# A transformer layer on one core: q loads, x's split, batch 1's reciprocals and step 30 put in another order

## The reference

```
h = layernorm(x)
q = h @ Wq (32 heads of 32);  k, v = h @ Wkv (one head of 32 each)
a = softmax(q k^T * scale + slopes * (pos_k - pos_q), causal) v
x = x + a @ Wo
w = (6-bit codes of qweight - zero_point) * scale
x = x + layernorm(x) @ w^T + bias
```

## Time and profile before

| | |
|---|---|
| median of 3 runs (range) | 864.13 us (860.87 to 867.29) |
| the profiled execution, its span | 865.46 us, 863.7 us |
| mean granted clock of TensorE | 0.979 of full |
| busy in the span: TensorE, VectorE, ScalarE, GpSimd | 824.9, 580.6, 379.6, 434.0 us |
| DMA | 126.35 MB, mean 146 GB/s |

### The profile page before, as it was taken

One profiled execution on the slowest core, in us unless ns is written; L12 is line 12 of the kernel. 1 busy time (PEld: TensorE's weight loads), 2 busy tenths in 40 slices (PEclk: granted clock), 3 DMA queues, 4 the chain that ended last, 5 costly groups with the idle time before them and its releaser, 6 DMA issues.

```text
span 863.7 us, 13629 instructions
## 1 busy us (share of the span) xinstructions
PE 824.9 (96%) x4616; PEld 591.6 (68%) x4616; DVE 580.6 (67%) x1582; ACT 379.6 (44%) x731; POOL 434.0 (50%) x320
## 2 busy tenths in 40 slices
PE   7999999989899999999999999995999999999988
PEld 4787878867655655565556555683887888888876
DVE  4866564656767878888888883215744878684876
ACT  3646436312466677667666664202411141041321
POOL 0000000000278888888888886425654378453555
PEclk9999999998999999999999999996999999999999
DMA  9767676594546545664566535234035532510112
GB/s 334 256 204 221 212 255 206 170 232 124 151 115 148 146 132 143 147 158 109 156 161 158 146 104 201 60 110 159 33 116 181 168 122 95 173 49 1 49 49 98
DMA packets 70860, 126.35 MB, mean 146 GB/s; under 512 B 7444, under 2 KB 16692, under 8 KB 70456
## 3 DMA queue, kind: packets, MB, share of 16 engines
q1 hardware_dynamic: 70640, 125.23, 49.1%
q10 hardware_dynamic: 152, 0.27, 0.1%
HBM read 86.13 MB, written 38.94 MB: 145 GB/s over the span
## 4 chain that ended last, share of the span: by engine, by line
PE 67%; DMA 11%; DVE 7%; POOL 5%; issue 4%; ACT 4%; SPq 1%; DVEq 0%; POOLq 0%; ACTq 0%
PE p_st L868 10%; PE p_s L839 9%; PE p_o L879 9%; PE p_o L892 4%; PE p_s L939 4%; PE p_s L940 4%; PE p_s L941 4%; DMA inv<-inv_d 3%; DMA inv_b<-inv_d 3%; PE p_st L963 2%; PE p_st L964 2%; PE p_o L785 2%; PE p_o L788 2%; PE p_o L786 2%; PE p_st L939 2%
## 5 line engine op out<-in xcount | busy, mean ns | idle before, releaser
L1377 DVE CUSTOM_DVE_ANT_0 spill<-p_s,mask 128x128 bf16<-128x128 f32 (+3 forms) x512 | 223.2, 482 | 56.9 <-PE p_s L839 54.9
L612 POOL TENSOR_SCALAR_AFFINE_SELECT pt<-pt 128x512 f32<-128x512 f32 x128 | 81.9, 652 | 276.0 <-ACT pt L1111 276.0
L1111 ACT ACTIVATE pt<-p_st 128x512 f32<-128x512 f32 (+1 forms) x352 | 178.3, 559 | 86.1 <-PE p_st L868 85.7
L839 PE MATMUL p_s<-kst,xt 98*128 98x128 f32 (+3 forms) x512 | 150.3, 332 | 7.1 <-DVE mx L1377 5.8
L868 PE MATMUL p_st<-xt,kst 100*128 100x512 f32 (+1 forms) x352 | 140.7, 405 | 3.3 <-ACT pt L1111 2.9
L839 PEld LDWEIGHTS p_s<-kst,xt 98*128 98x128 f32 x512 | 99.1, 195 | 21.3 <-DVE mx L1377 8.5
L619 POOL TENSOR_TENSOR pt<-pt 128x1536 f32<-128x1536 f32 x32 | 111.8, 3492 | 2.7
L868 PEld LDWEIGHTS p_st<-xt,kst 100*128 100x128 f32 x352 | 66.7, 190 | 39.2 <-DVE ml L1384 18.1
L879 PE MATMUL p_o<-pt,vst 128*32 128x512 f32 (+3 forms) x1024 | 89.9, 445 | 0.0
L625 POOL TENSOR_TENSOR pt<-pt 128x1024 f32<-128x1024 f32 x32 | 76.9, 2403 | 0.0
L785 PE MATMUL p_o<-xt,wqh 128*128 128x512 f32 x136 | 55.7, 410 | 1.7 <-DVE wql L1291 1.7
(11 more groups left out here) (202 smaller groups left out, 1657.8 us busy)
## 6 DMA issues: line engine op xcount, KB each, us to landing
xt<-qh_d SPq DMA_DIRECT2D x64, 256.0 KB
xs<-in_x_t_dram SPq DMA_DIRECT2D x32, 256.0 KB, 5.8
qh_d<-qh SPq DMA_DIRECT2D x32, 256.0 KB, 3.1
ql_d<-ql SPq DMA_DIRECT2D x32, 256.0 KB, 4.0
xt<-ql_d SPq DMA_DIRECT2D x32, 256.0 KB
o_d<-o_st SPq DMA_DIRECT2D x32, 256.0 KB, 2.3
ob<-o_d SPq DMA_DIRECT2D x32, 256.0 KB, 4.1
xin<-in_x_dram SPq DMA_DIRECT2D x14, 512.0 KB, 8.4
```

The costliest lines, as they stand in the source:

```text
L839: pe.matmul(scores_of(n), qst[s % 4][0:R_MAX, j, qb * P:(qb + 1) * P], kst[0:R_MAX, b * S:b * S + keys], start=True, stop=True).then_inc(s ...
L1111: act.activation(pt[s % 2][:, j:j + heads, PT_AT[kb]:PT_AT[kb] + KB_LEN[kb]], p_st[:, place(k) % 3, 0:heads * KB_LEN[kb]].rearrange("p (j ...
L1377: dve.tensor_tensor_reduce(spill[:, SPILL_AT[qb]:SPILL_AT[qb] + keys], scores_of(n), mask[:, S - keys:S], 1.0, LOWEST, ALU.add, ALU.max, m ...
```

## The change

- SP, last batch: one `load_q` ahead of the stores, the others ahead of those of m = 2, 4 and 6, and that of step 3 at m = 6 instead of in step 0.
- VectorE and ScalarE, m = 7 of the first three batches: parts 6 and 7 of x are centred and split ahead of the q tile.
- Last q tile: ScalarE takes step 0's first two exponentials before its cast; VectorE's subtraction moves behind four maxima.
- Step 30: products 5 and 6 to its start, the low parts and product 7 behind `max_low`; `o_high(7)` and `o_low(7)` to step 31.
- Batch 1's outputs: all eight products on VectorE, 8 to 13 in step 31, 14 and 15 behind three evictions; eight broadcasts, six into places of their own (`inv_1`, which lies elsewhere in memory), the first six issued in step 31. The product is written over the reciprocals, so that `ob` comes free sooner. GpSimd keeps `add_x2` alone.
- The load of `scal` ahead of the wait for the last reciprocals, which `deviation(0)` waits for instead of the cast of `share_r`.
- MEAN of batch 0 from behind o(1,0) to behind four parts of o(1,1); SQUARES of the last batch from behind f(3,1) to behind f(3,2).

```diff
...
         sb = tensors(ctx)
         x2 = [None, sb("x2_odd", [P, CK, S])]
-        dev = sb("dev", [P, S])
+        share_r = sb("share_r", [P, P], F32R)
         scal = sb("scal", [P, 3 * CK])
         zs = sb("zs", [P, CK])
-        share_r = sb("share_r", [P, P], F32R)
+        dev = sb("dev", [P, S])
         sb("unused", [P, 224])
         x2[0] = sb("x2_even", [P, CK, S])
+        with ExitStack() as early:
+            inv_1 = tensors(early)("inv_1", [P, CK, S])
         yh = sb("yh", [P, CK, S], F32R)
...
             o_b = tensors(early)("o_b", [P, CK, 2, S], F32R)
         wi = sb("wi", [P, CK, CK, P], F32R)
-        with ExitStack() as early:
-            inv_1 = tensors(early)("inv_1", [P, CK, S])
         yl = sb("yl", [P, CK, S], F32R)
         xc = sb("xc", [P, 3, S])
...
         o_in = [sem(f"o_in{i}") for i in range(4)]
         inv_in = [sem(f"inv_in{i}") for i in range(2)]
-        inv_1_in = [sem(f"inv_1_in{i}") for i in range(2)]
+        inv_1_in = [sem(f"inv_1_in{i}") for i in range(6)]
         o_norm, o_hi, o_lo = (sem(n) for n in ("o_norm", "o_hi", "o_lo"))
         tile_done, evicted = sem("tile_done"), sem("evicted")
...
             return x2[t % 2][:, m, :]
+        def own_place(k):
+            return {CK: 0, CK + 1: 1, CK + 2: 2, CK + 3: 3, CK + 6: 4, CK + 7: 5}.get(k)
         def inv_turn(k):
-            return k if k < CK + 2 else k - (CK - 2)
+            return k if k < CK else k - 4 if k < 2 * CK else k - 6
         def inv_at(k):
-            return inv_1[:, k - CK, :] if CK + 2 <= k < 2 * CK else inv_b[:, inv_turn(k) % 2, :]
+            return inv_b[:, inv_turn(k) % 2, :] if own_place(k) is None else inv_1[:, own_place(k), :]
         def inv_landed(k):
-            if CK + 2 <= k < 2 * CK:
-                return inv_1_in[(k - CK) // 4], 16
+            if own_place(k) is not None:
+                return inv_1_in[own_place(k)], 16
             return inv_in[inv_turn(k) % 2], 16 * (inv_turn(k) // 2) + 16
+        def o_normal_at(k):
+            return inv_at(k) if k // CK == 1 else ob[:, k % 4, :]
         def xc_at(t, m):
...
                     load_codes(2 * b)
                     sp.wait_ge(q_done, CK * LASTB)
-                    for s in range(3):
-                        load_q(s)
+                    load_q(0)
                 for m in range(CK):
                     if not more and m in (6, 7):
                         store_max(m - 6)
+                    if not more and m in (2, 4, 6):
+                        load_q(m // 2)
                     n = CK * b + m
                     rows, cols = slice(m * P, (m + 1) * P), slice(b * S, (b + 1) * S)
...
             def attend(s):
-                if s + 3 < STEPS:
+                if 0 < s and s + 3 < STEPS:
                     at_least(sp, st_done, NU * s)
                     load_q(s + 3)
...
                 for k in range(CK):
-                    if k < 7 and s == max(17 + 2 * k, 19):
+                    if k < 7 and s == (17 + k if k < 2 else 17 + 2 * k):
                         load_inv(k)
                     if s == (19 + 2 * k if k < 4 else 14 + 2 * k):
...
                 if s == STEPS - 1:
                     for k in range(CK, CK + 4):
+                        load_inv(k)
                         load_o(k)
-                    load_inv(CK)
-                    load_inv(CK + 1)
+                    load_inv(CK + 4)
+                    load_inv(CK + 5)
                 if s > 0:
                     store_o(s - 1)
...
                     sp.wait_ge(wo_lo, HALVES)
                 sp.wait_ge(o_out, 16 * k + 16)
-                at_least(sp, o_lo, k - 3)
+                if CK + 4 <= k < 2 * CK:
+                    sp.wait_ge(o_norm, k - 3)
+                elif 2 * CK <= k < 2 * CK + 4:
+                    sp.wait_ge(o_norm, 2 * CK)
+                else:
+                    at_least(sp, o_lo, k - 3)
                 sp.dma_start(ob[:, k % 4, :], o_d[P * g:P * g + P, b * S:(b + 1) * S]).then_inc(o_in[k % 4], 16)
...
                 sp.wait_ge(inv_out, 16 * (b + 1))
-                at_least(sp, o_norm, CK + 1 + k - 2 * CK if 2 * CK <= k < 2 * CK + 2 else k - 1)
+                if own_place(k) is not None:
+                    sp.wait_ge(st_done, NU * (STEPS - 1 if own_place(k) < 4 else STEPS))
+                elif 2 * CK <= k < 2 * CK + 2:
+                    sp.wait_ge(o_lo, k - 3)
+                else:
+                    at_least(sp, o_norm, k - 5 if CK <= k < 2 * CK else k - 1)
                 src = inv_d[b].rearrange("(j r) q -> j r q", j=4)[:, g:g + 1, :].to_broadcast([4, 32, S])
                 sp.dma_start(inv_at(k), src).then_inc(inv_landed(k)[0], 16)
-            def load_inv_1(half):
-                sp.wait_ge(pv_done, STEPS)
-                src = inv_d[1].rearrange("(j r) q -> j r q", j=4)[:, 4 * half:4 * half + 4, :].rearrange(
-                    "j (a g) q -> j a (g q)", a=1).to_broadcast([4, 32, 4 * S])
-                sp.dma_start(flat(inv_1[:, 4 * half:4 * half + 4, :]), src).then_inc(inv_1_in[half], 16)
             def load_wi(m):
...
             for s in range(STEPS):
                 attend(s)
+            load_o(CK + 4)
+            load_o(CK + 5)
+            load_inv(CK + 6)
+            load_inv(CK + 7)
+            load_o(CK + 6)
+            load_o(CK + 7)
             store_o(STEPS - 1)
-            load_inv_1(0)
-            load_inv_1(1)
-            for k in range(CK + 4, 2 * CK):
-                load_o(k)
             load_x2(1, 0)
             load_x2(1, 1)
+            sp.dma_start(scal[:, :], rows).then_inc(rows_in, 16)
             sp.wait_ge(inv_done, 16 * B)
             sp.dma_start(inv_d[B - 1, :, :], sums[:, :]).then_inc(inv_out, 16)
-            sp.wait_ge(inv_out, 16 * B)
-            sp.dma_start(scal[:, :], rows).then_inc(rows_in, 16)
             for k in range(2 * CK, 2 * CK + 4):
...
                 add(s, 1)
-            for k in range(CK, CK + 3):
-                o_normal(k)
-            add_x2(0, 1)
-            add_x2(0, 2)
-            for m in range(3, CK):
-                for k in (CK + 2 * m - 3, CK + 2 * m - 2):
-                    if k < 2 * CK:
-                        o_normal(k)
+            for m in range(1, CK):
                 add_x2(0, m)
             for t in (1, 2, 3):
...
             for t in (1, 2, 3):
                 for m in range(CK):
-                    out_tile(t, m)
-                    if (t, m) == (1, 0):
-                        over_features(0, MEAN)
+                    for c in range(CK):
+                        out_part(t, m, c)
+                        if (t, m, c) == (1, 1, 3):
+                            over_features(0, MEAN)
                     if m == 4:
                         over_features(t - 1, YSUM)
...
             for m in range(CK):
                 ffn_tile(LASTB, m)
-                if m == 1:
+                if m == 2:
                     over_features(LASTB, SQUARES)
...
                         act.activation(mv[:, 0, 3:4], eps[:, 0:1], ACT.Exp).then_inc(table_in, 1)
+                    if n == CK * B - 1:
+                        exponentials(0, 0)
+                        exponentials(0, 1)
+                    if more and m == CK - 1:
+                        for c in CENTRE[m]:
+                            x_high(b + 1, c)
                     act.wait_ge(q_freed, n + 1)
                     at_least(act, q_out[m % 2], 32 * (4 * b + m // 2))
...
                     if 0 < b < LASTB and m == TURN_M[b]:
                         take_stats(b + 1)
-                    if more:
+                    if more and m < CK - 1:
                         for c in CENTRE.get(m, ()):
                             x_high(b + 1, c)
...
                 if k == 0:
                     at_least(act, pv_done, s - 1)
+                    if s == 0:
+                        act.wait_ge(q_done, CK * B)
                 act.activation(pt[s % 2][:, j:j + heads, PT_AT[kb]:PT_AT[kb] + KB_LEN[kb]],
                                p_st[:, place(k) % 3, 0:heads * KB_LEN[kb]].rearrange("p (j q) -> p j q", j=heads),
...
                     if k == TURN_AT and 0 < s < STEPS - 1:
                         max_high(s + 1)
-                    exponentials(s, k)
+                    if (s, k) not in ((0, 0), (0, 1)):
+                        exponentials(s, k)
                     if k == 0 and s % GROUPS == 1 and s > GROUPS:
                         take_sums(s // GROUPS - 1)
...
                     if k == 3 and s in (21, 23, 25, 27, 29):
                         o_high((s - 21) // 2)
-                    if s == STEPS - 2 and k in (3, 6, 9):
+                    if s == STEPS - 2 and k in (3, 6):
                         o_high(k // 3 + 4)
+                    if s == STEPS - 1 and k == 3:
+                        o_high(7)
...
                 if k == 3 * CK:
                     act.wait_ge(tile_done, tile_at("o", 2, CK - 1) + 1)
```

(50 more changed lines are left out.)

## The result

The changed kernel took 832.32 us in the median of 4 runs (831.53 to 833.71), the kernel before 865.71 (860.87 to 868.90). The ratio is 0.9621, its 95% interval 0.957 to 0.9671. In a later comparison the same two gave 831.96 (6 runs) and 867.57 (11 runs), 0.96 (0.9574 to 0.9626). The forecast was 836.7, from 831 to 846: the time is inside, near the lower end, and 4.4 us better than forecast.

What follows compares the result with a forecast made beforehand. TensorE was taken as the bound, busy 824.9 of 863.7 us, leaving only its waits and half clock to save. Terms 3.2+0.6+3.9+2.1+16.7+2.3 = 28.8 off the profiled 865.5 gave 836.7 us, range 831 to 846.

Steps and rivals of the forecast that it cites:

- (a): Third q tile of the last batch: fewer loads ahead of the stores shorten TensorE's wait; 3.2 us, at most 5.1.
- (b): Batch borders: splitting x's parts first removes two TensorE waits of 0.77 us; 0.6 us, between 0.3 and 1.5.
- (c): Steps 0 and 1: earlier maxima, earlier q load for step 3, less half clock; 3.9 us, or 2.1 with the clock falling.
- (d): Step 31: moving `o_high(7)` there removes TensorE's wait for ScalarE; 2.1 us, at least 0.
- (e): Border to the output products: early broadcasts and products on VectorE leave TensorE no wait; 16.7 us.
- Rival 1: Border's wait moves on: GpSimd, slowed by VectorE's products or late squares, holds TensorE 2 to 4 us; 841, chance 0.13.
- Rival 3: Border: eight broadcasts go one after another at 13.00 us each, TensorE stands 45 us; 882, chance 0.03.
- Between (e) and (f) nothing moves: After the border, before the tail: GpSimd's 10.82 us wait near 657 hangs on loads of `wi` as before.
- (f): Tail: the later squares' matmul removes TensorE's 2.19 us wait and VectorE ends sooner; 2.3 us, between 1.5 and 3.5.
- Rival 2: Last batch: q loads at m = 4 and 6 still hold back stores, two waits of 5.5+1.9 us; 851.5, chance 0.05.
- rival 4: Last batch: VectorE's keys, not the stores, are the bound, so nothing is gained there; 840, chance 0.07.

Runs made afterwards that it cites:

- `e1_three_q_first`: Changed kernel with the first three loads of q back ahead of the last batch's first stores; 838.23 us.
- `e2_two_q_first`: Changed kernel with two loads of q instead of one ahead of the last batch's first stores; 833.96 us.
- `e10_small_steps`: Changed kernel with the last batch's third unpacking behind two maxima and `max_low(31)` ahead of products 5 and 6; median 831.01 us, 0.9591 of the kernel before.
- `e5_x_split_old`: Changed kernel with parts 6 and 7 of x split behind the seventh q tile again; 832.60 us.
- `e3_q3_late`: Changed kernel with the load of step 3's q issued in step 0 again; 838.89 us.
- `e7_gpsimd_products`: Changed kernel with batch 1's eight products back on GpSimd, the broadcasts staying early; 835.18 us.
- `e11_mean_old`: Changed kernel with the mean's sum back behind o(1,0); 831.87 us.
- `e8_broadcasts_late`: Changed kernel with the eight broadcasts issued only behind the last step, the last four loads of `o` behind them, products still on VectorE; 847.44 us.
- `e12_squares_old`: Changed kernel with the squares' sum set back one tile, behind the second tile from the last; 836.17 us.

## Why the forecast was near, and what it had wrong

**(a), 3.2 forecast, 4.8 in the profile.** The mechanism was right: the third load ahead of the stores held the store back (`e1_three_q_first` restores it, `e2_two_q_first` shows that two do not), the wait became 2.3 us as worked out, and VectorE is what is late next (`e10_small_steps` shortens the wait by moving VectorE's work alone). What failed is the sentence "The fall costs some 1.9 us ... I take the nearer row, the same place": the clock falls behind this wait in some executions and not in others, the same program once each way, and one row could not show that. Of the eleven profiles with this wait it stayed whole in four and fell in seven, for 1.55 us each, less than the 1.9 of the prediction. The profiled execution had the better case, so 1.6 of the 4.8 us are luck. 3.2 is the more frequent value; the upper bound that the prediction named was 5.1.

**(b), 0.6 forecast, 1.0 measured** (0.12 of the 1.15 is start-up; 0.8 by `e5_x_split_old`). Both waits of 0.77 went, for 0.90 and 0.99 us by the events. The next late thing is `mr`, with waits of 0.82 and 0.32 us in the same two batches, which give 0.63 and 0.42 back. The prediction had named this chain of the statistics and taken too much off for it.

**(c), 3.9 forecast, 3.7 measured.** The sum was right, and as a difference of the two profiles its terms are there too. I had added 0.8 for the order, 1.33 for the load and 1.8 for the clock; the waits give 0.63 (0.82 and 0.29 before, 0.48 now) and 1.33, and the rest is half clock. What does not hold is to take the terms as the worth of each edit. Undoing the load alone costs 5.4 us, undoing the order alone 4.3, each more than the 3.75 that both save. Of the 4.3, 0.6 are waits and the rest half clock, which may be chance; the order's own worth stays open. The 5.4 are more than chance: the wait of 3.69 us is longer than the 1.33 of before. The terms do not add, for the subtraction's new place delays the last store on SP, and a load behind it comes later than before (0.9 us in `e3_q3_late`). I had asked what each queue was moved past only for the load, not for the store that the moved subtraction feeds. Step 1 starts its output 9.58 us after step 0's (236.06, 245.64): the steady pace, under the 10.5 named.

**(d), 2.1 forecast, 1.7 measured.** The 2.12 us went, and the prediction said where it could come back: "What is next is `max_low(31)`, now behind the two products that took 1.27 us". I took the gap before it for enough. The step that failed is the duration: they took 2.63 us there, and 0.62 us of wait is the price. "SBUF — State Buffer" of the Trainium skill, section "SBUF: two separate sides", has a VectorE operation with two SBUF inputs and a GpSimd operation that reads SBUF exclude each other: whichever starts first keeps the shared ports for the whole instruction. Here GpSimd's sum started first and ends at 508.20, and 1.27 us from there is 509.47, 0.3 us short of the measured 509.78, which stays unexplained; in `e10_small_steps`, behind the sum, the same two take 1.27. The traces agree, and I should have used the rule for this term and not only for the margin.

**(e), 16.7 forecast, 16.69 measured,** and the working held as well as the number: o(1,1) is evicted at 581.32 instead of 609.93, 28.6 us sooner, and 16.5 of them are this stage's. The experiments name the cause: the early broadcasts with the loads of `o` around them, not the engine of the products (`e7_gpsimd_products`: 46.21 us either way), and not the mean's place (`e11_mean_old`: 46.21). Late, they bring back 13.2 us in `e8_broadcasts_late`, whose edit moves the last loads of `o` too, so the two are not told apart. The remaining 3.5 us are half clock. TensorE's waits in the stage add up to 10.64 us before (4.54, 1.27, 1.27, 3.56) and to 10.90 in `e8_broadcasts_late` (7.92, 0.53, 1.43, 1.02); but the clock was down longer, as the windows show (length, busy time of PE, granted clock, DMA share, GB/s), first two of before, then one of that run, behind which the clock is whole again:

```profile
588.00:600.00 12.00, 6.59 (x12) 0.53 0.15 56
600.00:606.00 6.00, 4.44 (x11) 0.51 0.61 186
```

```profile
575.00:583.00 8.00, 3.82 (x10) 0.57 0.21 79
```

Rival 1 fell with it: the seven products beside GpSimd made TensorE wait nowhere in step 31. Rival 3 needed 11.0 us a broadcast; they come every 2.64 us in `e8_broadcasts_late`, faster than the 3.6 of the forecast.

**"Between (e) and (f) nothing moves" was wrong by 1.4 us.** The broadcast behind the loads of `wi` took 13.00 us before and 11.57 now, in the chain of the changed kernel:

```profile
616.07 11.57 DMA inv_b<-inv_d
```

TensorE's wait of 1.69 us at 664.23 became 0.28 at 634.05. In other profiles of kernels with the same border it was 0.0 to 0.8 us. I took one sample of a transfer beside others for a constant.

**The steps, 0 forecast, 0.65 measured.** A wait of 0.37 us of TensorE for a load, at 430.08 in the profile before, has no counterpart. It was no part of the change, and a profile each does not say more.

**(f), 2.3 forecast, 3.8 measured.** I had TensorE end 3.8 us earlier and VectorE only 2.3, and took the later. TensorE's end was right (3.79), and the step that failed is VectorE's: "VectorE then has result 5 at 854.53+0.85 = 855.4". VectorE's six results before tile 6 took 11.52 us before (843.01 to 854.53) and 10.28 now. One of them waited 0.46 us and took 1.83 instead of 0.94 in the profile before, at 847.60. The same happens in one of the twelve experiments:

```profile
820.64 1.83 DVE L1553 SCALAR_TENSOR_TENSOR x_odd<-ob,scal,x_odd 128x512 f32<-128x512 f32 x1 [0.46 <-DVE ob L1547]
```

That is `e7_gpsimd_products`, whose edit is far from there, and its cause stays open. I had built on a disturbance of one profile; another 0.3 us is that the last two results take 3.22 us and not 2 x 1.75. Of TensorE's 3.8 us, 2.3 are the wait and 1.4 half clock, which by `e12_squares_old` need not have followed. So the move itself is worth 2.3 by that run, and 3.8 in the pair of profiles.

Rival 2 (later loads hold later stores) found no wait anywhere in the last batch beyond the third tile; rival 4 is excluded by the cast's releaser and by the 6 us that `e1_three_q_first` costs. That the total came out 5.1 us beyond the sum is, by the table: 1.6 in (a), 1.5 in (f), 1.4 at `wi`, 0.65 in the steps and 0.5 in (b) with the start-up, less 0.2 in (c) and 0.4 in (d). The 1.6 in (a) are clock, and 1.2 of the 1.5 in (f) the disturbance that VectorE was spared.

## What to carry to other kernels

Ask for a moved step which store or load hangs on its result, on which queue, and what stands behind that store: two edits that pay together can each, alone, cost more than making neither, as the single profiles of (c) have it. When a transfer is slow by its pattern (2.64 us for 256 KB on a quarter of the engines), issue it early; which engine consumes it mattered little here. (That it must be in pieces was not tried.) And where a wait is of some 2 us, count the half clock behind it as a range from nothing to its full price, not as one value.
